# A CIN interaction kernel: the Gram product in paired 64-row halves, three PSUM banks for ScalarE, a new split of the last block

## The reference

```
X1[b,h,d] = sum_jk W0[h,j,k] e[b,j,d] e[b,k,d]  + b0[h]
X2[b,h,d] = sum_jk W1[h,j,k] e[b,j,d] X1[b,k,d] + b1[h]
X3[b,h,d] = sum_jk W2[h,j,k] e[b,j,d] X2[b,k,d] + b2[h]
z = concat(sum_d X1, sum_d X2, sum_d X3)         # (512, 384)
y = relu(relu([z, dense] W_top1 + b) W_top2 + b) W_top3
```

## Time and profile before

| | |
|---|---|
| median of 3 runs | 654.07 us (651.15 to 656.03) |
| the profiled execution | 654.38 us, its span 652.5 us |
| TensorE busy | 617.7 us (95%) |
| VectorE busy | 581.6 us (89%) |
| ScalarE busy | 558.5 us (86%) |
| GpSimd busy | 470.9 us (72%) |
| DMA moved | 46.16 MB, mean 71 GB/s |

### The profile page before, as it was taken

How to read it: one execution, slowest core, us unless ns; L and a number is a source line. 1 busy time by engine, 2 the same in 40 slices (tenths; PEclk the granted TensorE clock), 3 DMA queues, 4 the chain that set the end, 5 groups by cost and what they waited for, 6 DMA issues and landing times.

```text
span 652.5 us, 14351 instructions
## 1 busy us (share of the span) xinstructions
PE 617.7 (95%) x2595; PEld 477.3 (73%) x2595; DVE 581.6 (89%) x1233; ACT 558.5 (86%) x1767; POOL 470.9 (72%) x442
## 2 busy tenths in 40 slices
PE   0389999999999999999999999999999999999998
PEld 0146788787878787878788787878787878876673
DVE  0549999999999999999999999999999999999980
ACT  3048899999999999999899989999999999999782
POOL 6778898979797989989798979798987656420000
DMA  7533404131222314040414132231405050000200
GB/s 228 135 78 88 125 19 126 34 105 53 79 81 49 109 21 137 9 137 17 126 32 121 39 91 67 67 91 39 120 8 149 1 150 5 12 18 1 65 1 0
DMA packets 44274, 46.16 MB, mean 71 GB/s; under 512 B 20896, under 2 KB 27264, under 8 KB 44233
## 3 DMA queue, kind: packets, MB, share of 16 engines
q1 hardware_dynamic: 38482, 43.59, 23.0%
q0 software_dynamic: 5120, 1.32, 2.4%
q10 hardware_dynamic: 631, 0.74, 0.4%
HBM read 44.30 MB, written 1.31 MB: 70 GB/s over the span
## 4 chain that ended last, share of the span: by engine, by line
PE 88%; issue 4%; DVE 4%; POOL 1%; ACT 1%; DMA 1%; DVEq 0%
PE ya L528 12%; PE ya L530 12%; PE ya L529 12%; PE yd L528 9%; PE yd L530 8%; PE yd L529 8%; PE misc L511 5%; PE acc L500 4%; PE acc L499 3%; PE acc L501 3%; PE acc L504 2%; DVE chain L651 2%; POOL emb L390 1%; PE yd L611 1%; PE yd L609 1%
## 5 line engine op out<-in xcount | busy, mean ns | idle before, releaser
L779 ACT ACTIVATE prods<-ya,x0t 128x128 f32<-128x128 f32 x1472 | 452.0, 519 | 40.8 <-PE ya L530 37.8
L651 DVE SCALAR_TENSOR_TENSOR chain<-yd,x0t,chain 128x128 f32<-128x128 f32 x768 | 218.2, 343 | 4.9 <-remote 4.0
L390 POOL DMA_INDIRECT emb<-in_tables,rows x160 | 158.4, 990 | 35.4 <-issue 24.3
L528 PE MATMUL ya<-w1h,x1h 128*128 128x512 f32 (+1 forms) x384 | 166.4, 433 | 3.2 <-ACT prods L779 2.1
L437 POOL TENSOR_TENSOR prod0l<-prod,prod0h 120x512 fp32r<-120x512 f32 x98 | 127.6, 1302 | 47.8 <-ACT prod0h L788 47.2
L529 PE MATMUL ya<-w1l,x1h 128*128 128x512 f32 (+1 forms) x384 | 147.5, 384 | 0.0
L530 PE MATMUL ya<-w1h,x1l 128*128 128x512 f32 (+1 forms) x384 | 147.2, 383 | 0.0
L305 POOL TENSOR_TENSOR prod<-tiles,x0a 120x512 f32<-120x512 f32 x105 | 137.3, 1308 | 12.5 <-issue 4.2
L666 DVE TENSOR_REDUCE x2t<-prods 128x128 f32<-128x1792 f32 x64 | 129.2, 2019 | 2.4 <-issue 0.3
L666 DVE TENSOR_REDUCE prods<-prods 128x128 f32<-128x1536 f32 x64 | 111.7, 1746 | 0.1
L528 PE MATMUL yd<-w1h,x1h 128*128 128x512 f32 x256 | 102.5, 400 | 1.9 <-DVE prods L651 1.6
(11 more groups left out here) (102 smaller groups left out, 620.9 us busy)
## 6 DMA issues: line engine op xcount, KB each, us to landing
tiles<-x_rows SPq DMA_DIRECT2D x236, 78.0 KB
x0a<-x_rows SPq DMA_DIRECT2D x45, 80.0 KB
emb<-in_tables,rows POOLq DMA_INDIRECT x160
w<-in_w SPq DMA_DIRECT2D x3, 832.0 KB, 5.6
w<-in_w SPq DMA_DIRECT2D x13, 192.0 KB
tiles<-x_rows SPq DMA_DIRECT2D x32, 42.0 KB
x<-x_rows SPq DMA_DIRECT2D x16, 78.0 KB
x<-x_rows SPq DMA_DIRECT2D x16, 77.8 KB
```

The lines of the kernel that those rows point to most:

```text
L390: pool.indirect_dma_start(emb[:, c % 2, fo * D:(fo + 1) * D], None, a["tables"], bass.IndirectOffsetOnAxis(ap=rows[:, c, fo:fo + 1].bitcas ...
L528: pe.matmul(out, x1h[:, c % 2, xs], w1h[:, cols], start=True, stop=False)
L651: dve.scalar_tensor_tensor(out, product, x, run if step else b1[:, :], ALU.mult, ALU.add).then_inc(yd_used, 1)
L779: mm = act.activation(prods[:, :, slot_of(q) + i], ya[(NA * g + k) % YA][:, i * H:(i + 1) * H], ACT.Copy, scale=turned(c)[:, g * F1 + j:g ...
```

## The change

Seven edits go together.

1. **Columns in halves.** The 512 columns of a chunk are ordered by halves of 16 samples, each (d, sample), in DRAM as well: `scratch` has the shape (chunk, 2, 40, 256). A group is still every fourth column, so its rows 0 to 63 are four samples and rows 64 to 127 four others. Each load of a row of 2 KB becomes two of 1 KB, and the store goes in pieces of 16 numbers instead of 32.
2. **Row tiles for Gram.** The block diagonal needs only four samples (160 columns) per half. A Gram is two matmuls of 64 rows by 160 columns, one per half, written to two banks (`pair`, of which `misc` is the first).
3. **Pairs.** `gram_groups` takes two groups at once: groups 0 and 1 of a chunk after block (2,6), groups 2 and 3 after block (0,6) of the next. ScalarE copies them out after blocks 7 and 8 there. `diag` has four buffers.
4. **ya has three banks instead of four**, to make room for the second bank of `pair`.
5. **The last two blocks.** Block 8 (VectorE) has three fields and block 9 (ScalarE) four. VectorE has 15 steps per group instead of 16, ScalarE 24 fields instead of 23, and the second reduction 15 slots instead of 14.
6. **x1 and x1h.** x1 is written with d innermost, and x1h is written straight from `acc0`, no longer from x1.
7. **Two copies of x0** instead of three: both transposes of the turn have 78 rows.

```diff
-XB = 3
+XB = 2
+SIZES = (JB,) * (BLOCKS - 2) + (JB - 1, JB)
+FIRSTS = tuple(sum(SIZES[:q]) for q in range(BLOCKS + 1))
-YA, YD = 4, 2
+YA, YD = 3, 2
+DIAGS = 4
-        scratch = nc.dram_tensor("x0_rows", (CHUNKS, FP, COLS), F32, kind="Internal").ap()
-        acc0, misc = ps("acc0"), ps("misc")
+        scratch = nc.dram_tensor("x0_rows", (CHUNKS, 2, FP, HCOLS), F32, kind="Internal").ap()
+        acc0, pair = ps("acc0"), ps("pair", (P, 2, 512))
+        misc = pair[:, 0, :]
...
 def store_x0(x):
-                by_row = chunk_rows(x).rearrange("(f o) n -> f (o n)", f=FI)
-                for i, cols in enumerate((slice(0, FT * COLS), slice(FT * COLS, FO * COLS))):
-                    sp.dma_start(by_row[:, cols].rearrange("f (p b) -> p f b", b=CB),
-                                 xt[0:(cols.stop - cols.start) // CB, i, :].rearrange("p (f b) -> p f b", f=FI),
+                by_row = scratch[x, :, :, :].rearrange("h (f o) n -> (h f) (o n)", f=FI)
+                for i, cols in enumerate((slice(0, FT * HCOLS), slice(FT * HCOLS, FO * HCOLS))):
+                    sp.dma_start(by_row[:, cols].rearrange("q (p b) -> p q b", b=CB // 2),
+                                 xt[0:(cols.stop - cols.start) // (CB // 2), i, :].rearrange("p (q b) -> p q b", b=CB // 2),
...
 def load_x0(x):
-                    sp.dma_start(x0[g * F:(g + 1) * F, 0:COLS - g], chunk_rows(x)[0:F, g:COLS]).then_inc(x0_in, 16)
+                    sp.dma_start(in_halves(x0[g * F:(g + 1) * F, :])[:, :, 0:HCOLS - g], chunk_rows(x)[0:F, :, g:HCOLS]).then_inc(x0_in, 16)
...
 def block_diagonal(c, g):
-                wait_done(pool, g_done, n - 1)
+                wait_done(pool, g_done, n - DIAGS + 1)
-                pool.tensor_tensor(diag[:, n % 2, :, :], row.to_broadcast([P, GB, F1]),
-                                   mask.to_broadcast([P, GB, F1]), ALU.mult).then_inc(diag_ready, 1)
+                pool.tensor_tensor(diag[:, n % DIAGS, :, :], row.to_broadcast([P, HB, F1]),
+                                   mask.to_broadcast([P, HB, F1]), ALU.mult).then_inc(diag_ready, 1)
...
 def turn_x0(c):
                 pe.transpose(misc[:, 0:XB * F], by_group[:, 0, :], const[0:XB * F, C_ID:C_ID + XB * F])
-                pe.transpose(misc[:, XB * F:GROUPS * F], by_group[0:F, XB, :], const[0:F, C_ID:C_ID + F]
+                pe.transpose(misc[:, XB * F:2 * XB * F], by_group[:, XB, :], const[0:XB * F, C_ID:C_ID + XB * F]
                              ).then_inc(x0t_done, 1)
...
-            def gram_group(n, g):
-                pe.wait_ge(sums_done, 2 * n + 2)
-                pe.wait_ge(diag_ready, n + 1)
-                wait_done(pe, g_ready, n)
-                pe.matmul(misc[:, 0:GB * F1], x2t[:, g % 2, :],
-                          diag[:, g % 2, :, :].rearrange("p b j -> p (b j)"),
-                          start=True, stop=True).then_inc(g_done, 1)
+            def gram_groups(ns):
+                pe.wait_ge(sums_done, 2 * ns[-1] + 2)
+                pe.wait_ge(diag_ready, ns[-1] + 1)
+                wait_done(pe, g_ready, ns[0])
+                for i, n in enumerate(ns):
+                    for h in range(2):
+                        half, cols = slice(h * HROWS, (h + 1) * HROWS), slice(i * HB * F1, (i + 1) * HB * F1)
+                        mm = pe.matmul(pair[:, h, cols], x2t[half, n % 2, :],
+                                       diag[half, n % DIAGS, :, :].rearrange("p b j -> p (b j)"), start=True, stop=True)
+                mm.then_inc(g_done, len(ns))
...
-                        if q == G_AFTER and (g or prev):
...
+                        if q == G_AFTER and g == 0 and prev:
+                            pe.wait_ge(x0t_ready, min(c + 2, CHUNKS))
+                            gram_groups((GROUPS * c - 2, GROUPS * c - 1))
+                        if q == G_AFTER and g == 2:
+                            if lay:
                                 pe.wait_ge(x0_ready, c + 3)
-                            gram_group(GROUPS * c + g - 1, (g - 1) % GROUPS)
+                            gram_groups((GROUPS * c, GROUPS * c + 1))
+                        if q == G_AFTER and g == 3 and c == CHUNKS - 1:
+                            gram_groups((GROUPS * c + 2,))
...
 def sum_dims(c):
-                dve.tensor_reduce(z[:, bass.ds(c * CB, CB)].rearrange("p (g b) -> p g b", g=GROUPS),
-                                  x1[:, :].rearrange("p (g d b) -> p g b d", g=GROUPS, d=D), AX.X,
+                dve.tensor_reduce(z[:, bass.ds(c * CB, CB)].rearrange("p (g h b) -> p h b g", g=GROUPS, h=2),
+                                  x1[:, :].rearrange("p (h b g d) -> p h b g d", h=2, g=GROUPS, d=D), AX.X,
                                   ALU.add).then_inc(z_sums, 1)
...
 def evacuate_x1(c):
-                act.activation(x1[:, :].rearrange("p (g n) -> p g n", g=GROUPS),
-                               acc0[:, :].rearrange("p (n g) -> p g n", g=GROUPS), ACT.Identity, bias=bias[:, 0:1]).then_inc(x1_ready, 1)
-                act.wait_ge(x1_ready, c + 1)
-                act.activation(x1h[:, bass.ds(c & 1, 1), :].rearrange("p c n -> p (c n)"), x1[:, :],
-                               ACT.Copy).then_inc(x1h_ready, 1)
+                act.activation(x1[:, :].rearrange("p (h q d) -> p h d q", h=2, d=D),
+                               acc0[:, :].rearrange("p (h d q) -> p h d q", h=2, d=D), ACT.Identity, bias=bias[:, 0:1]).then_inc(x1_ready, 1)
+                act.activation(x1h[:, bass.ds(c & 1, 1), :].rearrange("p c (g n) -> p (c g) n", g=GROUPS),
+                               acc0[:, :].rearrange("p (n g) -> p g n", g=GROUPS), ACT.Identity, bias=bias[:, 0:1]).then_inc(x1h_ready, 1)
...
-                        if q == G_AFTER + 1 and (g or prev):
-                            evacuate_gram(GROUPS * c + g - 1)
+                        if q == G_AFTER + 1 and (g == 2 or g == 0 and prev):
+                            evacuate_gram(GROUPS * c + g - 2, 0)
+                        if q == G_AFTER + 2 and (g == 2 or g == 0 and prev):
+                            evacuate_gram(GROUPS * c + g - 1, 1)
+                        if q == G_AFTER + 1 and g == 3 and not nxt:
+                            evacuate_gram(GROUPS * c + 2)
```

More of the change, by code:

```diff
@@ L38 @@
 GROUPS = CB // GB
+HB = GB // 2
+HROWS = P // 2
+HCOLS = COLS // 2
 R0 = F + 1
@@ L54 @@
 C_MASK = 0
-C_ID = C_MASK + GB
+C_ID = C_MASK + HB
 C_ALL = C_ID + P
@@ L64 @@
 NA0, ND0 = OWNERS[:HALF].count("A"), OWNERS[:HALF].count("D")
-YA, YD = 4, 2
-assert NA * GROUPS % YA == 0 and ND * GROUPS % YD == 0 and JB * BLOCKS >= F > JB * (BLOCKS - 1)
+YA, YD = 3, 2
+DIAGS = 4
+assert NA * GROUPS % YA == 0 and ND * GROUPS % YD == 0 and FIRSTS[-1] == F
 CHAINS = 2
-STEPS = JB * ND
+D_SIZES = tuple(size for size, owner in zip(SIZES, OWNERS) if owner == "D")
+STEPS = sum(D_SIZES)
 S_HALF = JB * NA0
@@ L104, in fields_of, with steps_through @@
 def fields_of(q):
-    return range(JB * q, min(JB * q + JB, F))
+    return range(FIRSTS[q], FIRSTS[q + 1])
 def slot_of(q):
-    return JB * OWNERS[:q].count("A")
+    return sum(size for size, owner in zip(SIZES[:q], OWNERS) if owner == "A")
+def steps_through(n, k):
+    n, k = (n, k) if k >= 0 else (n - 1, k + ND)
+    return STEPS * n + sum(D_SIZES[:k + 1])
 def uses_before(i, ring, x):
@@ L188, in build @@
         x2t = sb("x2t", [P, 2, H])
-        diag = sb("diag", [P, 2, GB, F1])
+        diag = sb("diag", [P, DIAGS, HB, F1])
         gram = sb("gram", [P, F1, B])
@@ L274, in chunk_rows, with in_halves @@
         def chunk_rows(c):
-            return scratch[bass.ds(c, 1), :, :].rearrange("c r n -> (c r) n")
+            return scratch[bass.ds(c, 1), :, :, :].rearrange("c h r n -> r (c h) n")
+        def in_halves(x):
+            return x.rearrange("p (h n) -> p h n", h=2)
         def turned(c):
@@ L293, in load_tile @@
             for row, a, b in segments(i):
-                engine.dma_start(tiles[a:b, i % L0_TILES, :],
-                                 chunk_rows(x)[row:row + b - a, :]).then_inc(tile_in[i % L0_TILES], 16)
+                engine.dma_start(in_halves(tiles[a:b, i % L0_TILES, :]),
+                                 chunk_rows(x)[row:row + b - a]).then_inc(tile_in[i % L0_TILES], 16)
         def multiply0(engine, x, i):
@@ L306, in multiply0 @@
                                  ALU.mult).then_inc(prod0_ready, 1)
-        hid, hid2 = (acc0, ya[0], ya[1], ya[2]), (yd[1], ya[3])
+        hid, hid2 = (acc0, ya[0], ya[1], ya[2]), (yd[1], pair[:, 1, :])
         block = ctx.enter_context(nc.Block())
@@ L639, in multiply_add @@
                 for i, j in enumerate(fields_of(q)):
-                    step = JB * k + i
+                    step = sum(D_SIZES[:k]) + i
                     wait_done(dve, yd_used, STEPS * n + step - CHAINS + 1)
@@ L643, in multiply_add @@
                     x = turned(c)[:, g * F1 + j:g * F1 + j + 1]
-                    run = chain[:, step % CHAINS, :]
+                    run = chain[:, (g * STEPS + step) % CHAINS, :]
```

(9 more changed lines are left out.)

37 lines of the change are left out of this document (17 added, 20 removed).

## The result

The changed kernel takes 659.64 us (median of 10 runs, 656.70 to 661.52). The kernel before took 656.13 on the same chips (10 runs, 651.15 to 657.70). The ratio is 1.0056, with a 95% interval of 1.0041 to 1.0070: slower by 3.7 us by the ratio (3.5 between the medians), which is within 1%. The forecast was 662.6, in a range of 645 to 671; the likeliest class by its chances, slower by over 1%, did not come. The profiled execution took 659.91 us, its span 658.0.

A forecast was written before the change was run, and what follows sets the result against it. The prediction took TensorE to set the pace, with VectorE delaying it once per chunk. Its terms, -5.7 + 3.4 - 3.8 + 13.0 + 1.1 + 0.7 - 0.5 = +8.2, on 654.4 gave 662.6 us, range 645 to 671.

The forecast's parts named there:

- A: Turn of x0 on TensorE: 78-row transposes remove both changes of row size, -0.41 us per steady chunk, -5.7 us in all.
- B: Gram on TensorE: a pair in 64-row halves costs 0.12 us more than two Grams, +3.4 us over 28 pairs.
- wholly side by side: Rival: both Gram halves run together, a pair takes 0.95 us, B becomes -3.6, 655.6 us in all; chance 0.18.
- second rival: The rival "wholly side by side" for the Gram halves: no change in time, 655.6 us; chance 0.18.
- C: TensorE's wait for VectorE before the yd block in group 0: 0.27 us per chunk goes, -3.8 us.
- D: Three ya banks: group 0's first block waits for ScalarE's block q=5 of group 3, +13.0 us.
- late and on-time chunks: Two kinds of chunk in D, by when ScalarE ends q=5: seven late at 1.25 us, seven on time at 0.6.
- credit of 0.19 for x1h: In D, ScalarE in group 3 gains the 0.19 us that x1h waited for x1.
- E: Start: VectorE waits for the first tile behind the store in smaller pieces, +1.1 us (0 to 2).
- F: Chunk 0: with three banks TensorE waits for ScalarE one block earlier, three matmuls of 0.23 us, +0.7 us.
- G: Last chunk, where TensorE waits for VectorE in every group: 0.14 us less in each of four, -0.5 us.

The follow-up runs named there:

- e2: The kernel before with two copies of x0, so both turn transposes have 78 rows: 649.51 us, ratio 0.9992 to the kernel before.
- e10: The kernel before with the new split of the last two blocks and two copies of x0: 653.19 us, ratio 0.9954 to the kernel before.
- e1: The kernel before with three ya banks instead of four, nothing else changed: 650.04 us, ratio 1.0003 to the kernel before.
- e3: The changed kernel with x1 written contiguously and the sums over d reading with a stride: 653.77 us, ratio 1.0057 to the kernel before.
- e4: The changed kernel with x1h written first and x1 only after block (3,7): 651.63 us, ratio 1.0025 to the kernel before.
- e5: The changed kernel with the Gram pairs moved to groups 1 and 3: 645.70 us, ratio 0.9926 to the kernel before.
- e7: The kernel before with only the column order in halves, 64-byte store pieces and 1 KB loads: 650.08 us, ratio 1.0002 to the kernel before.
- e9: The kernel before with only the new split, block 8 three fields and block 9 four: 654.35 us, ratio 0.9979 to the kernel before.
- e6: The changed kernel with each pair's matmuls issued lower halves first, then upper halves: 654.20 us, ratio 1.0061 to the kernel before.
- e12: The changed kernel with one Gram, still in halves, after block 6 of every group instead of pairs: 659.48 us, ratio 1.0046 to the kernel before.
- e8: The changed kernel with the old split, block 8 four fields and block 9 three: 652.35 us, ratio 1.0043 to the kernel before.

## Why the prediction was right or wrong

- **A, the turn: the mechanism right, the term too large.** -0.31 per chunk, not -0.41. The two short transposes stream 0.07 each, and the load behind the second (0.19 long, begun at 322.19) holds the next block back. And in e2 and e10 this gain reached the chunk with nothing: the sum booked it in full.
- **B, Gram: the step that failed.** The forecast had a pair 0.12 dearer than two Grams; it is 0.14 cheaper (0.94 against 1.08), -3.9 us over 28 pairs where +3.4 were summed. The rival "wholly side by side" was right with its 0.95. The argument against it, that two parts of one half are in order, was true and no objection: each has its partner in the other half. The Trainium skill's rule of the second rival (TensorE: Matmul & The Clock Gate, Part 3, "Measured speedup vs the span model") holds here; the trace agrees: two parts of 160 columns, one in each half, take a step of 0.135 together. With this term and A set right, the sum is 8.2 + 1.4 - 7.3 = +2.3.
- **C, VectorE's hole.** It went as forecast, -0.27. The forecast named nothing in its place; a hole of 0.21 in group 1 came, between ScalarE's block 7 and VectorE's block 8, some +3 us over 14 chunks.
- **D, the ring: the size and the place right, the two kinds of chunk wrong.** 0.97 was measured where 0.93 was the mean of the terms, and it waits for ScalarE at group 0, as said. But the late and on-time chunks, 1.25 and 0.6, are not to be seen: nearly all wait 0.93 to 1.12. The credit of 0.19 for x1h was taken by the strided write of x1 (+0.47), which the forecast didn't price. And "three banks" is not the cause by itself: alone it costs 0 (e1), and relieved of 0.55 to 0.78 (e3, e4) TensorE waits for VectorE instead. The condition that the forecast named, ScalarE's block q=5 of group 3 against TensorE's arrival, holds in all eight kernels with three banks (the figures are under e5). What it missed is that the arrival can be moved at no cost: e5 puts 0.94 us of TensorE's work ahead of it. The changed kernel with four banks was not run, as its eight banks are all taken, so what a fourth would save is not shown.
- **E, the start: failed.** The first product, forecast near 27.8, begins at 25.61 in the profile after, earlier than in the one before (26.73). The smaller pieces alone change nothing (e7).
- **F and the start.** Of the 5.5 us between the profiled spans, 2.1 lie before the layout of chunk 0. ScalarE stands there 5.2 us with no engine named, TensorE behind it, and behind TensorE's idle time (2.85 us busy in eight) the mean granted clock is 0.82 and then 0.75, part of the stretch at the lower of its two levels (1.2 GHz), where before it is 1.00, the 2.4 GHz level. This is not the ring: e9, with four banks, shows 0.87 and 0.91 in the same stretches, and e6, with three, shows 1.00. The windows of after and of e9:

```profile
42.00:50.00 8.00, 2.85 (x11) 1.81 (x9) 0.59 (x3) 1.94 (x7) 6.34 (x7) 0.82 0.38 101
50.00:58.00 8.00, 7.21 (x23) 5.52 (x24) 7.32 (x16) 6.49 (x25) 3.03 (x5) 0.75 0.33 97
```

```profile
42.00:50.00 8.00, 4.11 (x15) 3.02 (x14) 3.82 (x9) 2.89 (x12) 4.45 (x6) 0.87 0.38 105
50.00:58.00 8.00, 8.00 (x29) 5.75 (x29) 7.15 (x18) 6.17 (x23) 5.96 (x6) 0.91 0.49 136
```

  The pause isn't the change's own either: ScalarE stands 4.5 us at the same place before. In the profiles of e9 to e12, on the slower of the three chips, chunk 0's layout begins at 61.55 to 64.17; in those of e1 to e8, with the change or without, at 55.70 to 58.01, and ScalarE has no such pause in e1 or e6. What it waited for the trace doesn't name, and it stays open. F's +0.7 is not to be seen: TensorE's wait for ScalarE in chunk 0 is 2.08 with three banks and 2.13 with four.
- **G** was not tested by itself; the whole tail is within 0.2 us of before.
- **The chunk.** 35.6 was forecast, 35.29 came. Counted by the rows: turn -0.31, two pairs -0.28, the hole of group 0 -0.27, ring +0.97, the new hole +0.21 make +0.32 against +0.19 measured. The table's work column puts the saving 0.13 higher than turn and pairs: the load behind the old Gram's wait for x2t (0.07) is in it, and the rest I can't place.
- **How much was luck.** The sum of +8.2 stands against +3.7. B was 7.3 too dear and E 1.1; against them stand 1.4 too much credit in A, 3 for the hole that nobody foresaw and about 1 that the ring cost beyond its 13.0. That the time came so near is owed in part to errors that cancel.
- **The wrong picture.** The prediction added terms to one engine's path and gave a single releaser to each wait. The experiments with a turn or a split alone show that these terms don't add. TensorE (34.1), ScalarE (34.5) and VectorE (33.1) are now within 1.4 us of each other in a chunk, and what couples them are two and three banks, some blocks of slack. So a sum over the chunk says little; what counts is, at each hand-over of a bank, whether its reader is done when TensorE comes.

That the wait is due to where TensorE's work stands, and not to how much there is, is shown by e5 (work moved, nothing else), and by e12 from the other side: 0.80 more work in a chunk of the same length. e2, e3, e4, e8 and e10 show that time won at one hand-over is lost at the next, to VectorE. That the last 0.53 of e5 belongs to VectorE alone is read from its row, not tried.

## What to carry to other kernels

Where engines are within a few per cent of each other and coupled by a few buffers, make the account per stretch as long as the buffers' slack, not per iteration: work taken from a stretch where the other engines are full is given back as a wait. Before crediting a saving, ask in which stretch it lies and who is next; before giving up a change with a new wait, find the two instructions that meet there and try to put work between them. Here the same change was 0.6% slower than before with its pairs in even groups and 0.7% faster in odd ones.
